# Opening re-ordered: norm weights spread and first row turned by TensorE, W2's logarithm and W1's products ahead

## What is computed

```
def _ternary_quant(w):
    s = jnp.mean(jnp.abs(w))
    wq = jnp.round(jnp.tanh(w / (s + EPS))) * jnp.arctanh(s)
def _linear_bit(x, w, g):
    xq = _act_quant(_rmsnorm(x, g))
    wq = _ternary_quant(w)
    return jnp.einsum('bsd,od->bso', xq, wq)
swish = jax.nn.silu(_linear_bit(x, w1, g1))
h = swish * _linear_bit(x, w2, g2)
return _linear_bit(h, w3, g3)
...
x = x + _L0_xattn_ref(_layernorm(x), ctx_2048, mask)
x = x + _L0_ffn_ref(_layernorm(x), w1, g1, w2, g2, w3, g3)
```

## Time and profile before

| | us |
|---|---|
| median of 3 runs | 446.92 (446.89 to 447.14) |
| profiled execution | 447.09 |
| its span, first to last instruction | 445.1 |
| PE busy | 402.3 (90%) |
| DVE busy | 382.1 (86%) |
| POOL busy | 357.7 (80%) |
| ACT busy | 343.6 (77%) |

### The profile page before, as it was taken

The page is one execution under the profiler, slowest core; times in us unless marked ns, Lnnn a source line. Parts: engine busy times, 40 slices in busy tenths (PEclk is TensorE's granted clock), DMA queues, the critical chain, the costliest instruction groups (busy, mean ns, idle before and its releaser), DMA issues.

```text
span 445.1 us, 8348 instructions
## 1 busy us (share of the span) xinstructions
PE 402.3 (90%) x1898; PEld 182.9 (41%) x1898; DVE 382.1 (86%) x834; ACT 343.6 (77%) x619; POOL 357.7 (80%) x560
## 2 busy tenths in 40 slices
PE   8455872989899998999999999999999989999996
PEld 8142330334444443444434444444344443444443
DVE  5579897589898979997998979897999799798794
ACT  3679697686888789886998699878988697667661
POOL 0175989899878998888978987898889997899960
PEclk9776797899999999999999999999999999999999
DMA  6999931446677546843684557554784325354461
GB/s 252 398 335 401 316 110 24 129 91 128 145 182 147 119 94 165 199 95 89 183 188 93 119 144 187 129 118 98 177 186 104 90 68 115 77 99 103 105 97 71
DMA packets 110359, 66.40 MB, mean 149 GB/s; under 512 B 100736, under 2 KB 100864, under 8 KB 106752
## 3 DMA queue, kind: packets, MB, share of 16 engines
q1 hardware_dynamic: 110336, 66.14, 57.9%
HBM read 33.10 MB, written 8.39 MB: 93 GB/s over the span
## 4 chain that ended last, share of the span: by engine, by line
PE 53%; ACT 11%; DVE 10%; issue 8%; DMA 7%; POOL 6%; SPq 2%; DVEq 1%; ACTq 0%; POOLq 0%
PE S L1279 31%; PE DN L1312 16%; DMA stageB<-in_w2T 5%; DVE stageB L973 3%; PE R L1258 3%; ACT stageB L741 3%; ACT L696 2%; DVE hm L979 2%; ACT prob L696 2%; POOL stageB L549 2%; PE R L1225 1%; DMA stageB<-stageB 1%; ACT sg L749 1%; ACT junk_x L719 1%; DVE X L1010 1%
## 5 line engine op out<-in xcount | busy, mean ns | idle before, releaser
L549 POOL TENSOR_TENSOR stageB<-stageB,g3b 128x512 f32<-128x512 f32 x127 | 161.6, 1285 | 8.7 <-DVE stageB L973 5.4
L1279 PE MATMUL S<-W1q,q12T 128*128 128x512 f16 x512 | 135.6, 388 | 6.4 <-DVE W1q L1045 3.7
L1279 PE MATMUL S<-W2q,q12T 128*128 128x512 f16 x512 | 133.5, 384 | 1.2 <-DVE W2q L1045 0.5
L1312 PE MATMUL DN<-W3q,stageB 128*128 128x512 f16 x496 | 122.6, 381 | 0.9 <-issue 0.8
L749 ACT ACTIVATE sg<-S,asc 128x512 f32<-128x512 f32 x128 | 87.0, 683 | 26.9 <-PE S L1279 25.9
L973 DVE TENSOR_TENSOR stageB<-sg,S 128x512 f32<-128x512 f32 x128 | 86.2, 679 | 21.8 <-ACT sg L749 20.3
L979 DVE TENSOR_REDUCE hm<-stageB 128x1 f32<-128x512 f32 x127 | 86.0, 678 | 2.2 <-POOL stageB L549 2.1
L1279 PEld LDWEIGHTS S<-W1q,q12T 128*128 128x128 f16 x512 | 48.8, 100 | 74.9 <-issue 11.6
L1279 PEld LDWEIGHTS S<-W2q,q12T 128*128 128x128 f16 x512 | 50.4, 99 | 64.8 <-issue 2.7
L1312 PEld LDWEIGHTS DN<-W3q,stageB 128*128 128x128 f16 x496 | 47.9, 98 | 60.2 <-issue 3.1
L756 ACT ACTIVATE junk<-stageB 128x1024 bf16<-128x1024 f32 x64 | 67.3, 1052 | 4.2 <-DVE stageB L973 4.2
(11 more groups left out here) (129 smaller groups left out, 436.4 us busy)
## 6 DMA issues: line engine op xcount, KB each, us to landing
X<-in_x SPq DMA_DIRECT2D x8, 1024.0 KB, 5.8
out_x<-X SPq DMA_DIRECT2D x32, 256.0 KB, 2.7
xTs<-in_xT SPq DMA_DIRECT2D x7, 1024.0 KB, 7.3
X<-in_w1T SPq DMA_DIRECT2D x4, 1024.0 KB, 10.9
stageB<-in_w2T SPq DMA_DIRECT2D x4, 1024.0 KB, 19.4
X<-in_w3T SPq DMA_DIRECT2D x4, 1024.0 KB, 11.0
ctxr<-in_ctx SPq DMA_DIRECT2D x16, 128.0 KB, 3.0
ctxc<-in_ctx SPq DMA_DIRECT2D x8, 128.0 KB, 4.4
```

Of the source, the lines that this page charges most:

```text
L549: nc.gpsimd.tensor_tensor(gh[q][:, part], hp[:, part], g3b[:, part], ALU.mult).then_inc(s_gh_made, 1)
L1279: mm = nc.tensor.matmul(bank[n % 2][:, :], q12T[q][:, i * KD + k, :], w[:, n, k, :], start=(k == 0), stop=(k == KD - 1))
L1312: mm = nc.tensor.matmul(bank[:, :], src[:, k, :], W3q[:, k, :], start=(k == 0), stop=(k == KH - 1))
```

## The change

The two DMAs that spread g1 and g2 become two of one row each, queued right behind x into partition 0 of the buffers `sg`. TensorE spreads each row with a product of a row of ones into R, ACT copies both into `g12b`, and TensorE makes them ahead of the context's turn; the twenty products of ones are ten. Tile 0's rows `c12` are turned by eight transposes of TensorE (`turn_12`) and one copy of ACT (`turned_12`) in place of the DMA. On SP the context rows of batch 1 move behind W3's second quarter, and g3 needs no wait for tile 0. `logs` for W2 comes right behind W2's mean on ACT, with W2's series, choice and tile 0's value factor ahead of tile 0's first `gain_3` on POOL. `up` can make W1's products alone, and chunks 0 and 1 of tile 0 are made for W1 first. Of W2, POOL scales the third quarter and ACT the fourth (before, ACT the third and POOL the fourth). The opening's lists of ACT, DVE and POOL are re-ordered.

```
--- before.py
+++ after.py
@@ sync @@
             load_ctxc(0)
             load_x(0)
+            for i, g in enumerate((g1, g2)):
+                sp.dma_start(sg[i][0:1, :], g.partition_broadcast(1)).then_inc(s_gains_in, 16)
             for k in range(WC):
                 load_w(stageA, w1T, k, w_in[0][k])
                 if k == 1:
                     load_ctxr(0)
-                if k == 2:
-                    for i, g in enumerate((g1, g2)):
-                        sp.dma_start(g12b[:, i, :], g.partition_broadcast(P)).then_inc(s_gains_in, 16)
...
             load_ctxc(1)
-            load_ctxr(1)
-            transpose_12(0, 0)
             sp.dma_start(g3b[:, :], g3.partition_broadcast(P)).then_inc(s_gain3_in, 16)
             sp.wait_ge(s_w1_act, 1)
             load_w(stageA, w3T, 0, w_in[2][0])
             sp.wait_ge(s_w1_act, 2)
             load_w(stageA, w3T, 1, w_in[2][1])
+            load_ctxr(1)
@@ gpsimd @@
             def quantize_12(t):
                 pool.wait_ge(s_a_f, 2 * (t + 1))
-                if later(t):
-                    pool.wait_ge(s_q12_in, 16 * t)
+                if later(t, 2):
+                    pool.wait_ge(s_q12_in, 16 * (t - 1))
+                elif t == 1:
+                    pool.wait_ge(s_turn_12, 1)
...
+            weight_scale(1, stageB[:, :], W2f, 2, s_w2_pool)
             stage_a_root(1, 1)
-            weight_scale(1, stageB[:, :], W2f, 3, s_w2_pool)
-            quantize_12(1)
-            stage_a_worth_gate(1)
+            arctanh_series(1)
+            arctanh_choice(1, 2)
+            stage_a_worth_value(0)
             pool.wait_ge(s_gain3_in, 16)
             gain_3(0, 0, 0)
+            quantize_12(1)
+            stage_a_worth(1, 1)
             gain_3(0, 1, 0)
             stage_a_mean(2, 2)
@@ scalar @@
+            def turned_12():
+                act.wait_ge(s_turn_12, 1)
+                nc.scalar.copy(q12T[0][:, :, :].rearrange("p k q -> p (k q)"), q12P).then_inc(s_q12_turned, 1)
...
             table(0, ACT.Exp)
+            for i in range(2):
+                act.wait_ge(s_gains_ps, i + 1)
+                nc.scalar.copy(g12b[:, i, :], R[i][:, :]).then_inc(s_gains_made, 1)
             attention_ccT(0)
...
+            turned_12()
             stage_a_var(1)
+            logs(1, 2, 2)
+            weight_scale(1, stageB[:, :], W2f, 1, s_w2_act)
             table(2, ACT.Silu)
@@ tensor @@
+            def turn_12():
+                pe.wait_ge(s_ident_h, 1)
+                pe.wait_ge(s_c12_made, 2)
+                for k in range(HB):
+                    mm = nc.tensor.transpose(q12P[:, k * P:(k + 1) * P], c12[:, k * P:(k + 1) * P], ident16[:, :])
+                mm.then_inc(s_turn_12, 1)
...
-            for i in range(20):
+            for i in range(10):
                 nc.tensor.matmul(DN[:, 0:P], ones[:, :], ones[:, :], start=True, stop=True)
+            pe.wait_ge(s_gains_in, 32)
+            for i in range(2):
+                nc.tensor.matmul(R[i][:, :], ones[0:1, :], sg[i][0:1, :], start=True, stop=True).then_inc(s_gains_ps, 1)
             attention_ccT(0)
             turn_x()
...
-            up(0, 0, 0)
-            up(0, 1, 0)
+            up(0, 0, 0, 0, 1)
+            up(0, 1, 0, 0, 1)
+            up(0, 0, 0, 1, 1)
+            up(0, 1, 0, 1, 1)
             up(0, 2, 0)
             up(0, 3, 0)
             up(1, 0, 1)
             attention_ccT(1)
             up(1, 1, 1)
+            up(1, 2, 1)
             weight_total(2, s_w3_abs, WC)
-            up(1, 2, 1)
```

More of the change, by code:

```diff
@@ L545, in gain_3 @@
                     pool.wait_ge(s_c3_made, NHALF * (t - 2) + n * NHALF // NCH + 1)
-                elif n == 0:
-                    pool.wait_ge(s_w2_act, t + 1)
+                elif n == 0 and not later(t):
+                    pool.wait_ge(s_w2_act, 1)
                 part = slice(n * CH, (n + 1) * CH)
@@ L626, in _ @@
             gain_3(0, 2, 0)
-            arctanh_series(1)
+            stage_a_root(2, 2)
             gain_3(0, 3, 0)
-            stage_a_root(2, 2)
+            quantize_12(2)
+            stage_a_worth(2, 2)
+            stage_a_mean(3, 3)
             gain_3(1, 0, 1)
-            quantize_12(2)
-            stage_a_mean(3, 3)
+            stage_h_root(0, 0)
             gain_3(1, 1, 1)
@@ L807, in _ @@
             silu(0, 3, 0)
+            square(0, 0)
             stage_a_var(2)
@@ L810, in _ @@
             silu(1, 0, 1)
-            square(0, 0)
+            square(0, 1)
             attention_ccT(1)
+            silu(1, 1, 1)
             weight_abs(2, stageA, 3, s_w3_abs)
-            silu(1, 1, 1)
-            square(0, 1)
             silu(1, 2, 1)
+            attention_half(1)
+            quantize_3(0, 0, 0)
             weight_scale(2, stageA, W3f, 0, s_w3_act)
-            attention_half(1)
             silu(1, 3, 1)
             weight_scale(2, stageA, W3f, 3, s_w3_act)
-            logs(1, 3, 2)
+            quantize_3(0, 1, 0)
             attention_exp(1)
+            logs(2, 3, 3)
             stage_a_var(3)
-            quantize_3(0, 0, 0)
             attention_probT(1)
@@ L1077, in _ @@
             weight_scale(1, stageB[:, :], W2f, 0, s_w2_dve)
+            weight_clip(W1f, 1, s_w1_act, 2, s_w1_q)
             weight_clip(W2f, 0, s_w2_dve, 1, s_w2_q)
[L1079 removed]
+            weight_clip(W1f, 2, s_w1_pool, 1, s_w1_q)
             weight_clip(W2f, 1, s_w2_act, 1, s_w2_q)
             stage_a_gain(1)
+            gate(0, 0)
+            weight_clip(W2f, 2, s_w2_pool, 1, s_w2_q)
             stage_a_max(1, 1)
             stage_a_factor(1, 1)
[L1084 to L1086 removed]
             gate(0, 1)
             weight_clip(W1f, 3, s_w1_pool, 2, s_w1_q)
[L1089 removed]
+            weight_clip(W2f, 3, s_w2_act, 2, s_w2_q)
+            attention_x1(0, 1)
             gate(0, 2)
[L1091 removed]
             max_3(0, 0, 0)
+            stage_a_gain(2)
             gate(0, 3)
[L1094 to L1099 removed]
+            max_3(0, 1, 0)
+            stage_a_max(2, 2)
+            gate(1, 0)
+            stage_a_factor(2, 2)
+            max_3(0, 2, 0)
+            attention_cc(1)
             gate(1, 1)
[L1101 to L1102 removed]
             max_3(0, 3, 0)
+            stage_h_top(0)
+            stage_h_factor(0, 0)
             gate(1, 2)
             attention_xstat(1)
+            weight_mean(2, WC)
+            weight_scale(2, stageA, W3f, 1, s_w3_dve)
             gate(1, 3)
[L1107 to L1110 removed]
             weight_clip(W3f, 0, s_w3_act, 1, s_w3_q)
             weight_clip(W3f, 1, s_w3_dve, 1, s_w3_q)
[L1113 to L1114 removed]
+            max_3(1, 0, 1)
+            attention_softmax(1)
             weight_clip(W3f, 2, s_w3_pool, 1, s_w3_q)
             weight_clip(W3f, 3, s_w3_act, 2, s_w3_q)
+            max_3(1, 1, 1)
+            stage_a_gain(3)
             attention_norm(1)
[L1118 removed]
             attention_x1(1, 0)
@@ L1267, in weight_total, with up @@
                 nc.tensor.matmul(DN[:, 0:parts], ones[:, :], wabs[:, i, 0:parts], start=True, stop=True).then_inc(s_w_tot, 1)
-            def up(t, n, q):
-                if n == 0:
-                    pe.wait_ge(s_q12_in, 16 * (t + 1))
+            def turn_12():
[4 more added lines that the diff above has]
+                mm.then_inc(s_turn_12, 1)
+            def up(t, n, q, first=0, count=2):
+                if n == 0 and first == 0 and later(t):
+                    pe.wait_ge(s_q12_in, 16 * t)
+                elif n == 0 and first == 0:
+                    pe.wait_ge(s_q12_turned, 1)
                 for i, (bank, w, wq, done, used) in enumerate(((S1, W1q, s_w1_q, s_up1_ps, s_silu_made),
                                                                (S2, W2q, s_w2_q, s_up2_ps, s_hp_made))):
+                    if not first <= i < first + count:
+                        continue
                     if later(t) or n >= 2:
@@ L1328, in _ @@
             attention_readout(0, 1)
-            for i in range(14):
+            for i in range(16):
+                nc.tensor.matmul(xP[0][:, 0:P], ones[:, :], ones[:, :], start=True, stop=True)
+            turn_12()
+            for i in range(5):
                 nc.tensor.matmul(xP[0][:, 0:P], ones[:, :], ones[:, :], start=True, stop=True)
             weight_total(1, s_w2_abs, WC + 1)
-            up(0, 0, 0)
-            up(0, 1, 0)
+            up(0, 0, 0, 0, 1)
+            up(0, 1, 0, 0, 1)
+            up(0, 0, 0, 1, 1)
+            up(0, 1, 0, 1, 1)
             up(0, 2, 0)
```

42 lines of the change are left out of this document (9 added, 33 removed).

## The result

The changed kernel takes 458.33 us (median of 4 runs, 457.54 to 459.64) against 446.9 for the kernel before (446.22 to 447.14): 1.0261 times, 95% interval 1.0234 to 1.0288. The forecast was 455.9, slower, and its range ended at 458.5. The direction holds. The size is 2.4 us short, and the time lies on the upper edge: the median is just under it, two of the four runs are over it (458.61 and 459.64), and by the ratio it would be 446.92 x 1.0261 = 458.6. The profiled execution took 458.61, its span 456.6.

What follows compares the result with a forecast made beforehand. After 100 us TensorE is full; before it, a chain of waits through DVE, ACT and POOL bounds the start. Quantizing tile 3 comes 10.2 later, less 1.2 taken back: 447.09 + 9.0 = 456.1, less 0.17, 455.9 us; range 446.0 to 458.5.

Steps and rivals of the forecast that it cites:

- m: Moment when POOL has the mean of tile 2: 50.7 before, forecast at 58.5, 7.8 us later.
- W1's mean, +1.9: Opening: the gains' products delay the context's turn and all up to W1's mean by 1.9 us, up to 2.8.
- W2's reciprocal at 35.7: DVE, opening: reciprocal of W2's mean there at 35.7, as before, the first clip waiting for POOL's scaling of W1.
- POOL waits for DVE's whole run, 42.7 to 44.7: POOL's scaling of W2 waits out DVE's 5.5 us run of scaling, clips and gain products, then runs 42.7 to 44.7.
- m to V, 16.7: Stretch from tile 2's mean to W3's reciprocal in DVE's new order: 16.7 us, with gate (1,1) at 10.6.
- V: Moment of the reciprocal of W3's mean: 59.5 before, forecast at 75.2.
- V to Q, 20.7: Stretch from W3's reciprocal to quantizing tile 3: 20.7 us, POOL standing in front of tile 3's root for ACT's variance.
- Q: Moment when POOL starts to quantize tile 3: 85.7 before, forecast at 95.9, +10.2.
- 1.2 us taken back: TensorE's 1.16 us of idle time between 90 and 100 us was to be taken back, making +10.2 into +9.0.
- Faster: Rival: POOL gets its turn inside DVE's run, m at 49.3, time 443; decided at m = 57.4; chance 0.14.
- Overlapping waits: Rival: most of POOL's 14 us of idle time after m vanishes and DVE bounds; 446.9 to 451; chance 0.25.
- The change doesn't do what it says: Rival: W2's mean comes no sooner, the gains' products taking back the queue's gain; already in the sum, 454 were gains free.

Runs made afterwards that it cites:

- warm_apart: Changed kernel with twenty products of ones ahead of the gains' products instead of ten, and g2's row on partition 64 instead of 0: 453.31 us, ratio 1.0160.
- warm20: Changed kernel with twenty products of ones ahead of the gains' products instead of ten: 455.58 us, 1.0179 times the kernel before.
- late_gains: Changed kernel with the gains' products behind the scores, copied by DVE, and twenty products of ones again: 452.89 us, 1.0120 times the kernel before.
- late_clip: late_gains with DVE's first clip of W1 moved behind W2's mean: 451.44 us, 1.0108 times the kernel before.
- mix_gains: mix plus the moves of late_gains and late_clip: 442.97 us, 0.9918 times the kernel before.
- gains_first: Kernel before with only the one-row gain loads, TensorE's spreading ahead of the context's turn, ten products of ones and two ACT copies: 450.44 us, ratio 1.0073.
- v_early: Changed kernel with batch 1's context statistics and W3's total and mean made earlier: 455.45 us, 1.0190 times the kernel before.
- tail_old: Changed kernel with the opening's tail in the old order on DVE, ACT and TensorE, including the softmax ahead of tile 0's factor: 450.87 us, ratio 1.0099.
- root3_late: Changed kernel with POOL's root of tile 3 back behind W3's series and choice: 456.60 us, 1.0209 times the kernel before.
- mix: Kernel before with only W2's early logarithm, POOL's series in its idle time, choice and value factors where the series stood: 444.57 us, ratio 0.9947.
- series_late: Changed kernel with POOL's series, choice and value factors for W2 behind tile 2's mean and third gain_3: 457.91 us, 1.0238 times the kernel before.

## Why the direction was right and the size short

Two steps of the sum failed by much, in opposite directions: the price of the gains' products, and POOL's wait for DVE's run. Two more, behind m, add the rest.

**W1's mean, +1.9: wrong, +4.6.** This is the step that failed in the direction of the miss. It put the low clock in the wrong place: it took it for the gains' products, which ran at 0.92, and x's turn at half clock only for the upper bound of 2.8; the scores were in neither. The 1.6 at the context's turn came out near the forecast's 1.9 by luck, since the price at full clock, taken from the readout whose two products overlap (warm_apart), was 1.13 where 1.98 is right. Ten more products of ones give back 2.5 of the 4.6 (warm20). x's turn at half clock alone costs 1.7, so the bound of 2.8 was short as well; with 4.6 in its place the range would have ended near 460.3.

**W2's reciprocal at 35.7: wrong by the same term** (38.18; by late_gains the walk's own reason, the clip held up by POOL's scaling of W1, is right: 35.35).

**POOL waits for DVE's whole run, 42.7 to 44.7: wrong.** POOL's scaling took 3.45 (39.71 to 43.16): it waited 1.5 us, not 5.5. The Trainium skill, page "SBUF — State Buffer", section "SBUF: two separate sides", has the shared ports as a lock, and the forecast read from it that POOL gets a turn inside the run. By this row it does, behind DVE's scaling and one clip, and my choice against it was the worse one. In late_clip (2.40), mix_gains and gains_first (2.31 each) the scaling came nearer still to the 1.97 it needs alone. This error of 4 us hid the one above: the rest of the sum, 12.3 us, took 12.9, and m came within 0.7 by two errors of opposite sign.

**m to V, 16.7: 18.7.** Gate (1,1) was forecast at m + 10.6 and ended at m + 12.9. TensorE, idle 4.31 for the statistics, made the two products in 1.89 and 1.91 where I took 1.0 for one and hid the other beside silu: the clock again (granted 0.50). V itself bounds nothing (v_early). What counts behind it is where the softmax stands, as far as tail_old shows it.

**V to Q, 20.7: 20.9, right,** with the 8.15 us of POOL's idle time. Of these only 1.7 could be won (root3_late), since DVE's factor of tile 3, behind the readout, then comes last.

**1.2 us taken back: wrong, nothing was** (0.1). The idle slots behind Q moved with it.

The sum of the misses: -0.7 (m) + 2.0 (m to V) + 0.1 (V to Q, with rounding) + 1.2 = 2.6, against 458.61 - 456.1 = 2.5.

**The rivals.** "Faster" fell since m was 57.8, past its 57.4, with waits behind it. "Overlapping waits" fell too: it wanted most of POOL's 14 us of idle time behind m gone, and there are 18 (18.50 - 10.26 and 20.80 - 10.85 in the first two stretches above). "The change doesn't do what it says" was true in part: with the gains off the path W2's mean still came no sooner than before until the clip was moved (late_gains, late_clip).

## What to carry to other kernels

When a wait enters TensorE's list, price every short piece behind it at both clock levels, not only the moved one. Before a moment is used as a waypoint, ask what is released by it and last: V was forecast to 1.3 us and bounded nothing that Q waits for. Work made earlier is worth having where the engine that makes it idles (mix); put in front of tile 2's mean it moved waits about and changed the time by nothing that shows (series_late).
